# Seven blocks of transposing loads ahead of the stores, in a mixture-of-experts tail on one Trainium2 core

## The chip, the cores and the metric

The kernel runs on one core of one Trainium2 chip. The metric is the device time of one execution in microseconds (us); lower is better. The core has five engines with a sequencer each: PE (TensorE, matmuls, with its weight loads listed as PEld), DVE (VectorE), ACT (ScalarE), POOL (GpSimd) and SP (SyncE), which here only issues DMAs and waits on semaphores. A "q" behind an engine's name in a row (PEldq, SPq) marks an instruction of its sequencer.

## The reference

The input is x of 32 sequences of 256 tokens with 128 channels. Two layers are added to it in turn:

```
x = x + attn(layernorm(x))          # a gated linear recurrence (scan) with 192 channels
x = x + ffn(layernorm(x))           # the part below
def ffn(x):                         # 8192 tokens of 128 channels
    x = x + attention(layernorm(x)) # 16 heads of 8 channels, softmax over 256 keys
    m = layernorm(x)
    wts, idx = top_k(softmax(m @ Wg), 2)     # 2 of 8 experts for each token, weights normed
    h = gelu(m @ W1[e] + b1[e])              # 128 -> 512
    y = h @ W2[e] + b2[e]                    # 512 -> 128
    return x + sum over the 2 chosen experts of wts * y
```

## The kernel before, in words

The kernel goes through the scan layer, the attention of the first half of the sequences, the routing of that half, the attention and routing of the second half, and then the experts. This document is about the experts' stage, from about 818 us of the span to its end.

**Sorting by expert.** For each token and chosen expert POOL scatters a row into `xs` (expert_in) in DRAM with an indirect DMA, so that rows of one expert stand together. A row is 256 numbers of f16: the token's 128 channels as a high part and a low part. The rows are cut into `NBLK` = 80 blocks of `BS` = 256 rows, each of one expert, whose number stands in the table `blke`. Blocks 0 to 39 hold the first half of the tokens, 40 to 79 the second half. The second half's scatters still run while the first blocks are computed: POOL issues them as `down_done` counts up, and SP waits for all of them (`scattered[1]`) before its own block 32.

**One block.** SP loads the block with a transposing DMA into one of four buffers `XT[q]` (128 channels x 2 parts x 256 tokens, f16; it is a view of the tensor `arena`). PE makes `up(b)`: 12 matmuls of 256 columns with the expert's `w1h`, `w1l` into two PSUM banks. ACT makes `gelu(b)` in four instructions (line 854) into `G32`. DVE makes `split(b)`: a cast to f16 (line 1165) and a subtraction (line 1167). PE makes `down(b)`: 18 matmuls with `w2p` and the bias into a PSUM bank. DMA-ready output comes from one DVE reduction, `y_out(b)` (line 1172), into one of two buffers `YB`. SP stores it to `ys` (expert_out).

**The order on each engine** is written out by hand and runs over b with the helper `blocks`: blocks up to 3 and from 72 on are unrolled, and blocks 4 to 71 are a hardware loop with four blocks in a turn, q = 0 to 3. In its slot b each engine does the following.

- PE: reads the experts' numbers into registers (`value_load`, line 1476; two in slots q = 0, 1 and 2, one in q = 3), waits for `xt_in` of block b+3, for `gelu_done` of block b+1, for `gl_ready` of block b and for `yb_ready` of block b-2, and then issues `up(b+3)` and `down(b)` in turn. `up_done` and `down_done` are both raised at the slot's end. All of PE's matmuls go through one helper, line 1209.
- ACT: `gelu(b+2)`, as soon as `up(b+2)` is done.
- DVE: `y_out(b-1)`, which waits for `down(b-1)` and for the store of block b-3 to have landed, and then `split(b+2)`.
- SP: a load, then `store_block(b)`, which waits for `yb_ready`. All of SP's DMAs go into one queue.

The load in SP's slot b (line 446) is that of block b+4 into the buffer `XT[q]` that `up(b)` has read. It is issued behind `store_block(b-1)` (line 442), so behind `y_out(b-1)`. `exists(b)` is false only in the unrolled part for a block that there isn't.

**The end.** When all stores have landed, POOL gathers the second half's rows with 64 indirect DMAs (line 682), DVE combines them with `wts` and X, and SP stores the output. The first half's 64 gathers run beside blocks 41 to 78.

Of the kernel before, what the change touches and what calls it, by code (L numbers as in the profile page):

```python
# [63 lines left out]
def layer_kernel(nc, x, w_hg, b_hg, w_out, b_out, h0, g1, be1, g2, be2, wq, wk, wv, wo, wg, w1, b1,  # L64
# [8 lines left out]
    with ctx:  # L73
# [3 lines left out]
        def sem(name):  # L77
            return ctx.enter_context(nc.semaphore(name))
# [208 lines left out]
        up_done = sem("up_done")  # L287
# [30 lines left out]
        def blocks(eng, first, body, second_part=None):  # L318

            for b in range(first, 4):
                body(b, b % 4)
            cut = HBLK // 4 - 2
            for r0, r1 in ((1, cut), (cut, NBLK // 4 - 2)) if second_part else ((1, NBLK // 4 - 2),):
                if second_part and r0 == cut:
                    second_part()
                with eng.Fori(r0, r1) as r:
                    for q in range(4):
                        body(4 * r + q, q)  # L330
            for b in range(NBLK - 8, NBLK):
                body(b, b % 4)

        def exists(b):

            return not isinstance(b, int) or 0 <= b < NBLK
# [5 lines left out]
        def _(sp):  # L342
# [97 lines left out]
            def store_block(b, s):  # L440
                sp.wait_ge(yb_ready, b + 1)
                sp.dma_start(ys[bass.ds(b * BS, BS), :].rearrange("(h p) d -> p h d", p=P), YB[s])\  # L442
                  .then_inc(yb_out[s], 16)

            def load_block(b, q):
                sp.dma_start_transpose(XT[q], xs[bass.ds(b * BS, BS), :]).then_inc(xt_in[q], 16)

            def blocks_io(b, q):
                if exists(b + 4):
                    sp.wait_ge(up_done, b + 1)  # L450
                    load_block(b + 4, q)
                store_block(b, q % 2)

            sp.wait_ge(tab_ready, 2)
            sp.wait_ge(scattered[0], 32 * HN)
            for q in range(4):
                load_block(q, q)
            blocks(sp, 0, blocks_io, second_part=lambda: sp.wait_ge(scattered[1], 32 * (NT - HN)))

            for i in range(NG):  # L460
# [1116 lines left out]
```

## Time and profile before

| | us |
|---|---|
| median of 3 runs | 1243.0 |
| lowest and highest run | 1238.15, 1245.88 |
| the profiled execution's own time | 1232.73 |
| its span (first to last instruction) | 1230.9 |

| part of the span | us |
|---|---|
| before the experts | 0 to about 818 |
| expert blocks | about 818 to 1144 |
| gathers and combination of the second half | 1144 to 1230.9 |

PE is busy for 67% of the whole span, DVE for 70%, ACT for 49% and POOL for 37%. These are means over stages that differ, so they say little of the experts' stage. Rows give the time at which an instruction began and its duration; what stands in brackets behind a matmul is how long PE's array was idle before it and who is held to have ended that.

### The profile page before, as it was taken

Reading aid. Unit: us, or ns where it says so; the run is one execution under the profiler, and the core shown is the slowest. Engines: PE = TensorE matmul, PEld = TensorE weight load, DVE = VectorE, ACT = ScalarE, POOL = GpSimd, SP = SyncE. Lnnn points to the kernel's source line nnn. Section 1 sums busy time; section 2 is a strip of 40 time slices with the busy share of each in tenths; the row PEclk is TensorE's granted clock in tenths of the full one; section 3 lists DMA queues with packets and bytes.
Section 4 is the critical chain, followed back from the end, with each engine's and each line's share of the span. In section 5 each row is a group of like instructions: output and inputs, shape, how many; then the busy total and the mean of one; then the engine's idle time right before and its main releaser. Section 6 shows DMA issues by size and latency. Waiting matters only on the chain.

```text
span 1230.9 us, 25465 instructions
## 1 busy us (share of the span) xinstructions
PE 826.3 (67%) x8366; PEld 510.8 (41%) x8367; DVE 860.6 (70%) x1669; ACT 604.6 (49%) x1225; POOL 453.4 (37%) x552
## 2 busy tenths in 40 slices
PE   2577466688888884578888887547777777777000
PEld 1355344134443333423333333436666666666000
DVE  6788788777878847688888881856566666666722
ACT  3554278266767774227777775513333433343000
POOL 5800299011112214313333332724444033434675
PEclk9998799589989996559999997559999999999555
DMA  6900023211111210001211100013333233333432
GB/s 163 345 1 1 1 104 138 86 45 45 49 49 45 57 53 1 0 21 47 62 45 49 57 24 14 1 39 90 89 100 98 68 92 96 98 83 91 135 83 70
DMA packets 132071, 84.16 MB, mean 68 GB/s; under 512 B 54520, under 2 KB 117628, under 8 KB 131982
## 3 DMA queue, kind: packets, MB, share of 16 engines
q1 hardware_dynamic: 123790, 66.20, 18.6%
q0 software_dynamic: 8192, 16.79, 5.0%
q8 instruction: 54, 0.88, 0.3%
q14 instruction: 35, 0.29, 0.1%
HBM read 30.25 MB, written 41.94 MB: 59 GB/s over the span
## 4 chain that ended last, share of the span: by engine, by line
PE 44%; DVE 23%; POOL 9%; DMA 9%; issue 8%; ACT 4%; SPq 1%; ACTq 0%; DVEq 0%; POOLq 0%
PE bank L1209 41%; DVE arena L1024 9%; DMA arena<-expert_in 8%; POOL Z L682 2%; POOL HT L682 2%; POOL rr L473 2%; DVE arena L1172 2%; DVE mom L881 2%; POOL xh L477 2%; DVE arena L960 2%; PE bank L1389 1%; SPq L442 1%; ACT arena L854 1%; PE bank L1396 1%; PE bank L1213 1%
## 5 line engine op out<-in xcount | busy, mean ns | idle before, releaser
L1024 DVE TENSOR_REDUCE arena<-bank 128x2 f32<-128x512 f32 x512 | 337.3, 689 | 80.0 <-PE bank L1209 78.1
L774 ACT ACTIVATE arena<-bank 128x512 f32<-128x512 f32 x512 | 292.6, 596 | 131.2 <-PE bank L1209 128.1
L1209 PE MATMUL bank<-QK 32*128 32x256 f16 (+1 forms) x2048 | 204.8, 285 | 91.3 <-DVE arena L1024 69.2
L1209 PE MATMUL bank<-arena,w1h 128*128 128x256 f16 x640 | 170.9, 282 | 84.0 <-DMA arena<-expert_in 68.6
L640 POOL DMA_INDIRECT expert_in<-HT,idx x128 | 124.8, 975 | 266.7 <-PE bank L1209 239.2
L1209 PE MATMUL bank<-w2p,QK 128*128 x1280 | 221.6, 250 | 1.6 <-DVE arena L1172 1.6
L854 ACT ACTIVATE arena<-bank,b1s 128x256 f32<-128x256 f32 x320 | 125.5, 476 | 185.8 <-PE bank L1209 184.9
L1209 PEld LDWEIGHTS bank<-QK 31*128 31x128 f16 (+1 forms) x2048 | 63.3, 93 | 239.0 <-ACT arena L774 179.5
L1209 PE MATMUL bank<-arena,VA 128*32 128x256 f32 x2048 | 142.8, 398 | 1.4 <-ACT arena L774 1.4
L1209 PEld LDWEIGHTS bank<-w2p,QK 128*128 128x128 f16 x1280 | 126.0, 99 | 14.2 <-issue 1.7
L1209 PEld LDWEIGHTS bank<-arena,w1h 128*128 x640 | 64.2, 101 | 103.1 <-issue 96.8
L1165 DVE CAST QK<-arena 128x1024 f16<-128x1024 f32 x80 | 55.6, 696 | 70.4 <-ACT arena L854 70.4
L1213 PE MATMUL bank<-cst,xh 128*128 128x128 f32 x192 | 44.9, 386 | 86.7 <-ACT xh L813 32.6
L1167 DVE TENSOR_TENSOR QK<-arena,QK 128x1024 f16<-128x1024 f32 x80 | 98.0, 1226 | 2.7
L682 POOL DMA_INDIRECT Z<-expert_out,idx x64 | 61.9, 967 | 100.7 <-PE bank L1209 82.5
L473 POOL TENSOR_TENSOR rr<-vv,mhalf 128x8 f32<-128x8 f32 (+1 forms) x24 | 49.8, 2074 | 133.3 <-DVE vv L898 131.9
L1209 PE MATMUL bank<-arena,w1l 128*128 128x256 f16 x320 | 90.0, 281 | 0.0
L1172 DVE TENSOR_REDUCE arena<-bank 128x256 f32<-128x512 f32 x80 | 55.0, 689 | 44.1 <-PE bank L1209 42.2
L682 POOL DMA_INDIRECT HT<-expert_out,idx x64 | 62.0, 968 | 49.2 <-PE bank L1209 32.1
L1209 PEld LDWEIGHTS bank<-arena,VA 128*32 128x32 f32 x2048 | 54.7, 111 | 53.5 <-issue 23.2
L1213 PEld LDWEIGHTS bank<-cst,xh 128*128 128x128 f32 x192 | 31.3, 198 | 96.2 <-issue 49.4
L583 POOL COPY VA<-HT 128x128 f32<-128x128 f32 x64 | 16.8, 297 | 100.9 <-PE bank L1209 100.9
(150 smaller groups left out, 1220.4 us busy)
## 6 DMA issues: line engine op xcount, KB each, us to landing
QK<-qk_parts SPq DMA_DIRECT2D x96, 128.0 KB, 2.6
expert_in<-arena SPq DMA_DIRECT2D x40, 256.0 KB, 3.2
expert_out<-arena SPq DMA_DIRECT2D x80, 128.0 KB, 2.1
qk_parts<-arena SPq DMA_DIRECT2D x16, 512.0 KB, 2.8
X<-x SPq DMA_DIRECT2D x8, 512.0 KB, 5.8
wst<-w SPq DMA_DIRECT2D x16, 256.0 KB, 2.8
out<-arena SPq DMA_DIRECT2D x16, 256.0 KB, 2.4
expert_in<-HT,idx POOLq DMA_INDIRECT x128, 2.3
```

What stands on the lines that cost most here:

```text
L473: nc.gpsimd.tensor_tensor(rr[j % 2][:, 0:n, :], vv[j % 2][:, 0:n, :], mhalf[:, 0:n, :], ALU.pow)\
L477: return nc.gpsimd.tensor_scalar(dst, src, rr[j % 2][:, n, t:t + 1], nmr[j % 2][:, n, t:t + 1], ALU.mult, ALU.add)
L640: pool.indirect_dma_start(xs, bass.IndirectOffsetOnAxis(idx[:, k, n:n + 1], 0), MHL[:, n, :], None).then_inc(scattered[n // HN], 16)
L682: pool.indirect_dma_start(gat[k][:, n, :], None, ys[0:BS * BLK0[part + 1], :], bass.IndirectOffsetOnAxis(idx[:, k, n:n + 1], 0))\
L774: nc.scalar.activation(PT[t % 8], bank[2 + t % 2][:, :], ACT.Exp, scale=DH ** -0.5)\
L854: last = nc.scalar.activation(G32[s][:, BS * c:BS * c + BS], bank[2 + 2 * s + c // 2][:, BS * (c % 2):BS * (c % 2) + BS], ACT.Gelu_apprx_t ...
L1024: V.tensor_reduce(nmax[n % 2][:, :, 4 * j + g], bank[u % 2][:, :].rearrange("p (q t) -> p q t", q=2), AX.X, ALU.max, negate=True).then_inc ...
L1165: V.tensor_copy(GH[q], G32[q % 2]).then_inc(gh_own, 1)
L1167: V.tensor_tensor(GL[q], G32[q % 2], GH[q], ALU.subtract).then_inc(gl_ready, 1)
L1172: V.tensor_reduce(YB[s], bank[6 + s][:, :].rearrange("p (h k d) -> p h d k", h=2, k=2), AX.X, ALU.add) .then_inc(yb_ready, 1)
L1209: return nc.tensor.matmul(dst, lhsT, rhs, start=start, stop=stop)
L1213: last = nc.tensor.transpose(bk[:, P * t:P * t + P], src[:, t0 + t, :], ident)
```

## The change

SP sends its transposing loads earlier. Loads of blocks 0 to 6 are issued before the first store, blocks 4 to 6 each behind a wait for the buffer's last reader. In slot b the load is that of block b+7 into buffer (q+3) mod 4, behind a wait for `up(b+3)`, which reads that buffer last. The load still stands ahead of the store in the slot.

```
             def blocks_io(b, q):
-                if exists(b + 4):
-                    sp.wait_ge(up_done, b + 1)
-                    load_block(b + 4, q)
+                if exists(b + 7):
+                    sp.wait_ge(up_done, b + 4)
+                    load_block(b + 7, (q + 3) % 4)
                 store_block(b, q % 2)

             sp.wait_ge(tab_ready, 2)
             sp.wait_ge(scattered[0], 32 * HN)
-            for q in range(4):
-                load_block(q, q)
+            for b in range(7):
+                if b >= 4:
+                    sp.wait_ge(up_done, b - 3)
+                load_block(b, b % 4)
             blocks(sp, 0, blocks_io, second_part=lambda: sp.wait_ge(scattered[1], 32 * (NT - HN)))
```

The number of loads, their sizes, the four buffers and the one queue stay as they are.

## Rows read from the trace of the kernel before

**Rows 1.** The page: PE's clock in 40 slices, and the up-products' group.

```profile
PEclk9998799589989996559999997559999999999555
...
L1209 PE MATMUL bank<-arena,w1h 128*128 128x256 f16 x640 | 170.9, 282 | 84.0 <-DMA arena<-expert_in 68.6
```

**Rows 2.** Timeline of PE: first matmuls of slots 1 and 76.

```profile
832.43 0.28 PE L1209 MATMUL bank<-arena,w1h 128*128 128x256 f16 x1 [0.25 <-DVE QK L1167]
...
1131.80 0.28 PE L1209 MATMUL bank<-arena,w1h 128*128 128x256 f16 x1 [0.55 <-DMA arena<-expert_in]
```

**Rows 3.** Waits in 832 to 1132 us: total, times, longest.

```profile
PE bank L1209 <- DMA arena<-expert_in: 60.2, 62, 2.8
```

**Rows 4.** Timeline of PE: first matmuls of slots 32 to 37.

```profile
958.08 0.28 PE L1209 MATMUL bank<-arena,w1h 128*128 128x256 f16 x1 [1.80 <-ACT arena L854]
...
961.52 0.28 PE L1209 MATMUL bank<-arena,w1h 128*128 128x256 f16 x1 [0.51 <-DMA arena<-expert_in]
...
965.40 0.28 PE L1209 MATMUL bank<-arena,w1h 128*128 128x256 f16 x1 [0.95 <-DMA arena<-expert_in]
...
968.70 0.28 PE L1209 MATMUL bank<-arena,w1h 128*128 128x256 f16 x1 [0.37 <-DMA arena<-expert_in]
...
973.07 0.28 PE L1209 MATMUL bank<-arena,w1h 128*128 128x256 f16 x1 [1.45 <-DMA arena<-expert_in]
...
976.51 0.28 PE L1209 MATMUL bank<-arena,w1h 128*128 128x256 f16 x1 [0.50 <-DMA arena<-expert_in]
```

**Rows 5.** Timeline of SP: load of 36, store of 32, load of 37.

```profile
958.67 1.19 SPq L446 DMA_TRANSPOSE arena<-expert_in  x1
962.01 0.38 SPq L442 DMA_DIRECT2D expert_out<-arena  x1
962.61 1.19 SPq L446 DMA_TRANSPOSE arena<-expert_in  x1
```

**Rows 6.** Line 446, the loads, 832 to 1140 us: issue to landing.

```profile
DMA to landing us min/median/max: 2.6/2.9/4.5
```

**Rows 7.** Timeline of PE: last matmul of slot 32.

```profile
960.79 0.22 PE L1209 MATMUL bank<-b2h,ones 128*128 x1
```

**Rows 8.** Lines 1476, 1523, 958 to 973.2 us, PE's sequencer: ns, first, last.

```profile
L1476 PEldq TENSOR_LOAD <-blke x7: 297/302/310, 959.7 to 971.5; - x7
...
L1523 PEldq ALU_OP  x2: 32/34/36, 961.1 to 972.1; - x2
```

**Rows 9.** Line 316 (`used`), PE's sequencer, slot 33, then slot 34.

```profile
L316 PEldq EVENT_SEMAPHORE  x1: 51/51/51, 964.6 to 964.6; - x1
...
L316 PEldq EVENT_SEMAPHORE  x1: 51/51/51, 967.8 to 967.8; - x1
```

**Rows 10.** Timeline of PE: first matmuls of slots 47 and 48.

```profile
1015.36 0.28 PE L1209 MATMUL bank<-arena,w1h 128*128 128x256 f16 x1 [0.87 <-DMA arena<-expert_in]
...
1019.30 0.28 PE L1209 MATMUL bank<-arena,w1h 128*128 128x256 f16 x1 [1.01 <-DVE arena L1172]
```

**Rows 11.** Lines in 832 to 1132 us, DVE: busy, mean ns, idle before.

```profile
L1167 DVE TENSOR_TENSOR QK<-arena,QK 128x1024 f16<-128x1024 f32 x76 | 93.1, 1226 | 2.6
L1172 DVE TENSOR_REDUCE arena<-bank 128x256 f32<-128x512 f32 x76 | 52.4, 689 | 42.3 <-PE bank L1209 42.2
L1165 DVE CAST QK<-arena 128x1024 f16<-128x1024 f32 x75 | 52.2, 696 | 60.5 <-ACT arena L854 60.5
```

**Rows 12.** Timeline of ACT: the gelu after slot 32.

```profile
961.03 1.57 ACT L854 ACTIVATE arena<-bank,b1s 128x256 f32<-128x256 f32 x4 [3.09 <-PE bank L1209]
```

**Rows 13.** Timeline of PE: first matmuls of slots 68 and 69.

```profile
1098.32 0.28 PE L1209 MATMUL bank<-arena,w1h 128*128 128x256 f16 x1 [2.21 <-DMA arena<-expert_in]
...
1102.65 0.37 PE L1209 MATMUL bank<-arena,w1h 128*128 128x256 f16 x1
```

**Rows 14.** Windows: busy time of each engine, granted clock, DMA share, GB/s.

```profile
870.00:910.00 40.00, 29.70 (x305) 25.36 (x303) 26.96 (x32) 15.79 (x41) 19.19 (x20) 1.00 0.38 101
...
1098.00:1103.00 5.00, 4.68 (x33) 3.77 (x34) 1.83 (x3) 0.22 (x1) 0.71 (x1) 0.66 0.33 79
```

**Rows 15.** Line 442, the stores, 832 to 1145 us: issue to landing.

```profile
DMA to landing us min/median/max: 1.8/2.1/2.6
```

**Rows 16.** Timeline of POOL: first gather of the second half.

```profile
1144.53 0.94 POOL L682 DMA_INDIRECT Z<-expert_out,idx  x1 [5.40 <-DMA expert_out<-arena]
```

## Prediction, on record before the changed kernel was built

> **What bounds the kernel now.** I read the waits of the experts' stage first, then PE's timeline slot by slot, then PE's sequencer. The page's group of the up-products already says it: before them PE stood idle for 84.0 us, of which 68.6 ended with a load [rows 1]. In 832 to 1132 us, 75 slots from slot 1 to slot 76 [rows 2], PE waited 62 times for a load, 60.2 us in all [rows 3]. These slots take 1131.80 - 832.43 = 299.4 us, 3.99 each.
>
> The timeline shows how. The load of block 36 is issued at 958.67 and slot 33, which needs it, starts at 961.52, 2.85 later; that of block 37 is issued at 962.61 and slot 34 starts at 965.40, 2.79 later [rows 4, 5]. The loads land 2.6 to 4.5 us after issue, 2.9 in the median [rows 6]. So PE starts as the load lands. The load in turn is late because it stands behind a store in SP's order: the store of block 32 goes out at 962.01, the load 0.60 behind it [rows 5], and the store waits for `y_out`. After a slot ends, reduction, store, load and landing follow, 0.7 + 0.2 + 0.6 + 2.9 = 4.4 us, before the slot after the next can start. In slot 32 the first and last matmuls start at 958.08 and 960.79 [rows 4, 7]: the array needs 2.71 us plus one spacing of 0.06, so 2.77 a slot. That is what a reader might take as the new pitch, and it would be wrong, I think, by the next finding.
>
> **PE's sequencer is nearly as slow as the loads.** Slot 32 lasts 3.44 (958.08 to 961.52), slot 36 again 3.44 (973.07 to 976.51) [rows 4], and so do nine of the fourteen first-of-four slots from 12 to 64, whatever time the load was issued. A wait on a DMA does not repeat to 0.01 us. What repeats is the sequencer's own work between two slots: register arithmetic for the matmuls' addresses, then the reading of experts' numbers into registers, seven times in the group of slots 32 to 35, each 0.30 us [rows 8] plus some 0.45 of arithmetic and check about it, and the loop's branch. I take its time in each kind of slot from its last instruction ahead of the next slot. In slot 32 line 1523 runs at 961.1, 0.4 before the next slot starts [rows 4, 8]. In slot 33 the sequencer reaches its wait of line 316 at 964.6, in slot 34 at 967.8 [rows 9]; that is 3.1 and 2.4 after the slot's start, and 0.2 more pass from there to the first matmul (slot 32: line 1523 at 961.1, 0.1 to line 1527, 0.1 to line 316, 0.2 to 961.52). A slot of the fourth kind has the branch: slot 35 starts at 968.70 and line 1523 runs at 972.1, 3.4 later [rows 4, 8], and 0.4 to 0.5 follow. Slot 47 shows the whole: 1015.36 to 1019.30, 3.94 [rows 10]. So the four kinds cost the sequencer 3.44, 3.3, 2.6 and 3.94: **13.3 us for four blocks**, 3.32 each. Only the third kind is shorter than the array's 2.77, and there the sequencer runs 0.17 ahead and keeps it.
>
> **The change part by part.**
>
> The load's wait. The load of block b+7 goes out at the end of slot b and is needed at the start of slot b+4. Three slots lie between, 3 x 3.32 = 10.0 us, against 4.5 for the slowest landing [rows 6]. So all 62 waits of rows 3 should go. What is late next is the sequencer: 75 slots are 18.75 groups, 18.75 x 13.3 = 249.4 us, against 299.4. **Gain 50.0 us.** That is less than the 60.2 of waiting, since in slots of the first and fourth kind the wait lay beside sequencer work that stays.
>
> The other waits of PE's slot, at the new pitch. The gelu starts 0.03 after the slot's end and takes 1.57 [rows 12]; PE wants it one slot later, so 1.7 are left. DVE has 0.69 + 0.70 + 1.23 = 2.61 us of work in a slot of 3.32 [rows 11]. Its split ends 1.6 + 0.1 + 0.7 + 1.23 = 3.6 after the slot's end, so `y_out` begins some 0.3 late each time; PE asks for it, and for the split, a whole slot later. Cost 0; if the cover were gone it would be this 0.3 in each slot, 20 us.
>
> SP's added wait and the moved load. Each slot's load now waits for `up_done` of this very slot, and behind it in SP's order stand the store of block b and all later loads. `up_done` and `down_done` rise together, and the store needs `y_out` behind `down_done` anyway (0.69, [rows 11]). The load's issue takes 1.19 [rows 5], so the store goes out at about 1.5 us after the slot's end, up to 0.5 later than without the load. It lands 2.1, at most 2.6 later [rows 15], at 4.1; `y_out` wants the buffer two slots on, at 6.6. So 2.5 us of cover. SP has 1.19 + 0.38 of issue and under 1 us of steps in a slot: no bound. If a store's data queued behind the load's, even its worst landing of 4.5 [rows 6] would give some 6.2, still in time.
>
 No row of before has a store that close behind a load. By that rule the store would land at about 6 us, and the sum would stay at 50.0 us.
>
> The start and blocks 4 to 6. Slots before 832.43 did not wait for a load beyond the first; cost and gain 0. The scatters of the second half: 56 of them are released by 29 down-products, one per 1.72 us at the new pitch, and POOL needs about 1.25 for such a DMA (0.94 and a gap of 0.3, as in the gathers, [rows 16]). They keep up, and SP's wait before slot 32 would find three more blocks loaded. The tail from 1144.53 on, 64 gathers, hangs on the last store and only moves with it: 0.
>
> The clock. It is at 0.9 or more in the slices of this stage [rows 1], 1.00 (2.4 GHz) in 870 to 910 and 0.66 in 1098 to 1103, so partly at 1.2 GHz [rows 14]; slot 68 there takes 4.33 [rows 13] instead of 3.44, and slots 4, 8 and 72 are of this sort. These stretches came behind PE's longest pauses in the stage. I take them as gone, which the 13.3 already holds; if they stay, 4 x 0.9 = 3.6 us are lost.
>
> **Sum.** 1232.7 - 50.0 = 1182.7 for the profiled execution. The median of the runs is 1243.0, 10.3 above it, and I expect this distance again: **1193 us**. Own range: a group at 13.0 (0.3 of it being misread steps) gives 1187, one at 13.7 with the slow-clock slots 1204.
>
> **Rivals.**
>
> The array bounds (chance 0.05). If the sequencer's work were hidden because it runs ahead, a slot would be 2.77 to 2.82: 75 x 1.19 = 89 us less, 1154. For it: in slots of the third kind it does run ahead. Against it: an in-order sequencer needs 13.3 for four blocks whatever its lead, and 3.44 repeats. The skill's page TensorE: Matmul & The Clock Gate (section on the array as 16 of 32×32) gives PE a queue of 64, which lets it run that far ahead; by this alone the array would set the pace. The rows decide for me: depth hides a delay, not a lower rate.
>
> A new wait takes half of it (0.15). `y_out` waits for stores that land late, or DVE's lag of 0.3 grows through gelu and split. A pitch of 3.65, halfway between 3.32 and 3.99, gives 1243 - 25 = 1218. For it: three engines then have under 1 us of slack per slot. Against it: the slacks above of 1.7, 2.5 and more.
>
> The loads are not what ends the waits (0.05). Slot 32 starts 0.1 behind the end of a gelu by its label [rows 4]; if PE truly waited for the newest gelu, nothing would move: 1243. Against it: the code asks for a gelu one slot older, and slots 33 to 35 carry the load's label.
>
> Slower (0.04): stores behind loads in one queue. A store's landing L sets a pitch of (0.7 + 0.5 + L) / 2, since `YB` has two buffers. It costs something from L = 5.4 on (3.32 x 2 - 1.2), and all of the gain and more from 6.8 on. With L = 7.5 the pitch is 4.35: 75 x 0.36 = 27 us more, 1270. Against it: 2.6 at most now [rows 15], and DMA engines that are busy for 0.38 [rows 14], which the denser stage would raise to 0.46.
>
> **Chances.** Forecast 0.70, the array 0.05, half of it 0.15, nothing 0.05, slower 0.04, other 0.01. Range: the forecast's own and the rival at 1218 with its bounds, 1183 to 1222; the array's case, nothing and slower stay out, 0.14. This kernel can't tell changes under about 1% from none. Faster by over 1%: 0.91; within: 0.05; slower: 0.04.
>
> **What would show it.** Right: hardly a wait of PE for `expert_in`, slots of 3.44, 3.3, 2.8 and 3.8 in turn, slots 1 to 76 in about 250 us, the idle time before the up-products ended by nothing but issue. Loads landing 5 us or more before use. Wrong: a pitch of 2.8 (array), DVE's reduction ended by `expert_out` DMAs (stores), equal pitches of 3.6 with labels of ACT or DVE, or a granted clock below 1.00 in mid-stage.

## The result, and the profile after

| | before | changed |
|---|---|---|
| median, us | 1244.44 (4 runs, 1238.15 to 1251.02) | 1194.6 (4 runs, 1192.46 to 1201.33) |
| profiled execution's own time | 1232.73 | 1193.93 |
| its span | 1230.9 | 1192.1 |

The ratio is 0.9608, with a 95% interval of 0.9544 to 0.9672: 49.8 us faster by the medians, against 50.0 on record. That closeness is partly luck. The span fell by 38.8 only, and the parts of it, below, tell which terms were right. Medians here are of all executions of a kernel; ratios and their intervals leave out executions over 1.5% above the kernel's fastest.

The page and the waits of the expert stage come first. Behind the edit, lines of the kernel have moved by two: 1211 is the helper through which all of PE's matmuls go, 1169 DVE's subtraction, 1174 its reduction.

```profile
span 1192.1 us, 25516 instructions
...
L1211 PE MATMUL bank<-arena,w1h 128*128 128x256 f16 x640 | 167.6, 277 | 49.3 <-DVE QK L1169 24.9
```

Waits in 834 to 1089 us of the changed kernel (total, times, longest):

```profile
PEld bank L1211 <- issue: 47.4, 58, 1.4
...
PE bank L1211 <- DVE QK L1169: 24.9, 36, 1.1
...
PE bank L1211 <- issue: 11.4, 20, 1.0
```

No wait for `expert_in` is left of the 62 with 60.2 us in [rows 3]. The pauses of PE that are left carry the label of a DVE subtraction or "issue", which stands for time in which the engine waited for nothing that the profile shows; an experiment below tests the first of these labels. The timeline of PE, first matmuls of slots 1, 32 to 37 and 76, which answer to [rows 2, 4]:

```profile
834.24 0.28 PE L1211 MATMUL bank<-arena,w1h 128*128 128x256 f16 x1 [0.25 <-issue]
...
941.11 0.28 PE L1211 MATMUL bank<-arena,w1h 128*128 128x256 f16 x1 [1.00 <-DVE QK L1169]
...
944.55 0.28 PE L1211 MATMUL bank<-arena,w1h 128*128 128x256 f16 x1 [0.51 <-issue]
...
947.96 0.28 PE L1211 MATMUL bank<-arena,w1h 128*128 128x256 f16 x1 [0.48 <-DVE QK L1169]
...
950.72 0.27 PE L1211 MATMUL bank<-arena,w1h 128*128 128x256 f16 x1
...
954.64 0.28 PE L1211 MATMUL bank<-arena,w1h 128*128 128x256 f16 x1 [1.00 <-DVE QK L1169]
...
958.11 0.28 PE L1211 MATMUL bank<-arena,w1h 128*128 128x256 f16 x1 [0.54 <-issue]
...
1088.47 0.28 PE L1211 MATMUL bank<-arena,w1h 128*128 128x256 f16 x1 [0.60 <-issue]
```

The four kinds of slot take 3.44, 3.41, 2.76 and 3.92 us here. Only behind the third does the array go on without a pause. Slots 1 to 76 take 1088.47 - 834.24 = 254.2 us, 3.39 each, against 299.4. PE's sequencer (line 1525 is 1523 of before) in 941 to 956 us:

```profile
L1525 PEldq ALU_OP  x2: 32/34/36, 944.1 to 954.1; - x2
```

In slot 32 it gets to that line 3.0 us after the slot's start, in slot 35 at 3.4, as in [rows 8]. Its work takes as long as before; what is gone is the wait for loads that lay over it. SP's timeline for two slots:

```profile
940.14 1.19 SPq L446 DMA_TRANSPOSE arena<-expert_in  x1
941.64 0.38 SPq L442 DMA_DIRECT2D expert_out<-arena  x1
944.07 1.19 SPq L446 DMA_TRANSPOSE arena<-expert_in  x1
945.53 0.38 SPq L442 DMA_DIRECT2D expert_out<-arena  x1
```

Each load goes out at the end of a slot, its store 1.5 us behind it, as forecast. DVE's reduction hardly waits any more, and not for stores; the clock is full in the whole stage (0.98 in 832 to 1132 us before). DVE's reduction and the stage as a window, 834 to 1089 us (behind the window's length stand the busy times of PE, PEld, DVE, ACT and POOL with their instructions, then the granted clock, the DMA engines' busy share and GB/s):

```profile
L1174 DVE TENSOR_REDUCE arena<-bank 128x256 f32<-128x512 f32 x76 | 52.2, 687 | 3.9 <-PE bank L1211 2.8
```

```profile
834.00:1089.00 255.00, 217.41 (x2256) 189.04 (x2257) 192.36 (x227) 118.90 (x304) 119.84 (x116) 1.00 0.41 106
```

So the stage gave 299.4 - 254.2 = 45.2. Slot 1 began 1.8 later, and from slot 76 to the end 1192.1 - 1088.47 = 103.6 went by against 99.1 before, 4.5 more. 45.2 - 1.8 - 4.5 = 38.9, the difference of the spans up to rounding.

### The profile page after: what moved, and what is told of

Same layout as the page of the kernel before. It is cut to its first block, busy times and chain, and to the rows that moved or that the text cites. A ratio compares the mean times of both kernels' runs of the same rounds, so it can differ in the third digit from the quotient of the medians.

```text
span 1192.1 us, 25516 instructions
## 1 busy us (share of the span) xinstructions
PE 817.4 (69%) x8366; PEld 507.0 (43%) x8367; DVE 857.5 (72%) x1669; ACT 604.7 (51%) x1225; POOL 460.7 (39%) x552
## 4 chain that ended last, share of the span: by engine, by line
PE 47%; DVE 25%; POOL 12%; issue 9%; ACT 4%; DMA 1%; ACTq 1%; another core or an unknown queue 0%; SPq 0%; POOLq 0%; DVEq 0%
PE bank L1211 44%; DVE arena L1026 9%; POOL rr L475 3%; POOL xh L479 3%; DVE QK L1169 3%; POOL HT L684 2%; POOL Z L684 2%; ACT arena L856 2%; DVE arena L962 2%; DVE mom L883 2%; DVE QK L1167 2%; PE bank L1391 1%; PE bank L1398 1%; DVE xh L1080 1%; ACT arena L776 1%
## 5 line engine op out<-in xcount | busy, mean ns | idle before, releaser
L1211 PE MATMUL bank<-w2p,QK 128*128 x1280 | 215.8, 246 | 1.6 <-DVE QK L1169 1.6
L1211 PE MATMUL bank<-arena,w1h 128*128 128x256 f16 x640 | 167.6, 277 | 49.3 <-DVE QK L1169 24.9
L1211 PEld LDWEIGHTS bank<-w2p,QK 128*128 128x128 f16 x1280 | 124.0, 98 | 12.9 <-issue 1.7
L1215 PE MATMUL bank<-cst,xh 128*128 128x128 f32 x192 | 44.9, 386 | 88.1 <-ACT xh L815 32.6
L475 POOL TENSOR_TENSOR rr<-vv,mhalf 128x8 f32<-128x8 f32 (+1 forms) x24 | 49.8, 2076 | 132.8 <-DVE vv L900 131.4
L1169 DVE TENSOR_TENSOR QK<-arena,QK 128x1024 f16<-128x1024 f32 x80 | 98.0, 1226 | 2.7
L684 POOL DMA_INDIRECT Z<-expert_out,idx x64 | 64.3, 1005 | 79.4 <-PE bank L1211 60.9
L684 POOL DMA_INDIRECT HT<-expert_out,idx x64 | 64.8, 1013 | 37.5 <-PE bank L1211 19.0
L1215 PEld LDWEIGHTS bank<-cst,xh 128*128 128x128 f32 x192 | 31.3, 198 | 97.6 <-issue 49.5
```

The costliest lines, as they stand in the source:

```text
L475: nc.gpsimd.tensor_tensor(rr[j % 2][:, 0:n, :], vv[j % 2][:, 0:n, :], mhalf[:, 0:n, :], ALU.pow)\
L684: pool.indirect_dma_start(gat[k][:, n, :], None, ys[0:BS * BLK0[part + 1], :], bass.IndirectOffsetOnAxis(idx[:, k, n:n + 1], 0))\
L1169: V.tensor_tensor(GL[q], G32[q % 2], GH[q], ALU.subtract).then_inc(gl_ready, 1)
L1211: return nc.tensor.matmul(dst, lhsT, rhs, start=start, stop=stop)
L1215: last = nc.tensor.transpose(bk[:, P * t:P * t + P], src[:, t0 + t, :], ident)
```

## The experiments

There are twelve experiments, two of them repeats. A kernel's stage is the time from the first matmul of slot 1 to that of slot 76, its tail what comes behind. The runs went to three chips: the first four experiments below to one on which the kernel before had a median of 1240.28, the two with one reading more, the first unrolled run and the last experiment to one with 1240.69, the other four to one with 1235.14. Each ratio is to the kernel before on the same chip, and the stage is what is best compared between chips. The kernel before itself was profiled once.

**The changed kernel again.** No edit.

> The changed kernel once more, for a second profile. Both theories: 1195 us. The first profile lost 4.5 us behind the last expert slot and 1.8 ahead of slot 1 against the profile of before, at places where semaphores were seen 3 to 4 us late. If that belongs to the change it comes again at the same places; if it is an accident of one execution it is elsewhere or gone, and the span is up to 6 us shorter.

1197.89 us, ratio 0.9657 (0.9608 to 0.9706). The stage is 252.2 (835.82 to 1087.99), the span 1193.9, the tail 105.9. The waits of the tail (1087 to 1194 us):

```profile
DVE arena L1203 <- remote: 26.1, 6, 4.5
DVE arena L1195 <- remote: 18.8, 5, 4.5
```

"remote" stands for a wait to whose end the trace shows no releaser. Most of it costs nothing, since DVE would wait for gathers anyway: in the kernel before its waits for them in the tail are 47.4 us. POOL is done with the last gather 92.8 us after the first matmul of slot 76, and 92.3 in the kernel before; DVE's last combination ends at 103.1, against 96.4. In the first profile of the changed kernel one long wait of this kind stands in the tail, of 3.0 us, ahead of the very last combination. It is not the queue's doing: the experiment below that keeps the queue of before has it too, and the runs on the third chip don't. So the longer tail comes again, 105.9 here and 103.6 there, with its waits at places that vary, and not because of the change.

**A shorter lead.**

```
-                if exists(b + 7):
-                    sp.wait_ge(up_done, b + 4)
-                    load_block(b + 7, (q + 3) % 4)
+                if exists(b + 5):
+                    sp.wait_ge(up_done, b + 2)
+                    load_block(b + 5, (q + 1) % 4)
...
-            for b in range(7):
+            for b in range(5):
```

> Loads five blocks ahead instead of seven. A load is then issued about 1.3 us after the end of slot b-1 and needed at the start of slot b+2, 5.4 us later at a pitch of 3.4, against 2.9 for a landing. Sequencer theory (PE's sequencer sets the pitch once loads are not late): same as with seven, 1195 us. Rival (what helps is the long lead, since landings scatter up to 4.5 us): waits for loads come back, 1205 to 1220 us.

1206.23 us, ratio 0.9692 (0.9611 to 0.9774), which can't be told from 0.9657. The stage is 254.5 (843.46 to 1098.00), and one wait for a load is left in it:

```profile
PE bank L1211 <- DMA arena<-expert_in: 0.9, 1, 0.9
```

The profile's longer span comes mostly from before the experts: slot 1 started 9.2 us later than in the first profile of the changed kernel. At this pitch one block more of lead than before does all, within what these runs can tell, that three do.

**The store ahead of the load.**

```
             def blocks_io(b, q):
+                store_block(b, q % 2)
                 if exists(b + 7):
                     sp.wait_ge(up_done, b + 4)
                     load_block(b + 7, (q + 3) % 4)
-                store_block(b, q % 2)
```

> Seven blocks ahead, but the store of block b stands ahead of the load of block b+7. Sequencer theory: 1195 us, since neither store nor load ends a wait of PE or DVE. Rival (stores suffer behind the loads in the one queue): 5 us or more faster, and the store's landing, seen in what waits for it, earlier.

1199.43 us, ratio 0.9667 (0.9606 to 0.9729), stage 254.7. No difference that these runs could show: a store issued 0.3 us behind the issue of a load costs this kernel nothing. When the store lands doesn't stand in the profile.

**Less work for DVE.**

```
-                V.tensor_tensor(GL[q], G32[q % 2], GH[q], ALU.subtract).then_inc(gl_ready, 1)
+                V.tensor_tensor(GL[q][:, 0:2 * BS], G32[q % 2][:, 0:2 * BS], GH[q][:, 0:2 * BS], ALU.subtract)\
+                    .then_inc(gl_ready, 1)
```

> DVE subtracts for the first half of the columns of each block only, so the low part of half the hidden values is left out; DVE has 0.6 us less to do per slot. The waits after the change name this instruction as what ended PE's idle time, 36 times. Sequencer theory: the name is a coincidence of time, 1195 us. Rival (PE now waits for DVE's split): the pitch falls by 0.3 to 0.6 us, 1150 to 1172 us.

1195.59 us, ratio 0.9634 (0.9586 to 0.9683). The stage is 251.6 (856.83 to 1108.46, at a granted clock of 1.00; the profiled execution took 1214.38 us and came to slot 1 22.6 us later than the first profile of the changed kernel, with a granted clock of 0.83 up to there instead of 0.87). It is no shorter than the 252.2 of the same changed kernel beyond what profiles differ by, though DVE's subtraction went from 1226 ns to 692:

```profile
L1169 DVE TENSOR_TENSOR QK<-arena,QK 128x512 f16<-128x512 f32 x75 | 51.9, 692 | 2.6
```

The stage kept its pitch, and PE's idle time stayed, 34.5 us against 37.6, under other labels. These are its waits (lines have moved by one more: 1212 is PE's helper, 1175 the reduction):

```profile
PE bank L1212 <- issue: 23.8, 45, 1.0
PE bank L1212 <- DVE arena L1175: 8.0, 8, 1.1
PE bank L1212 <- DVE QK L1169: 2.7, 3, 1.3
```

The 24.9 us under the subtraction's name were a coincidence of time.

**One reading more per slot, changed kernel.** In PE's `experts`, the function of its slot:

```
                     if exists(x) and k not in known:
                         known[k] = expert_of(x)
+                if exists(b):
+                    expert_of(b)
```

> The changed kernel with one more reading of an expert's number into a register of PE in each slot; the result isn't used. Sequencer theory: 0.30 for the reading and 0.45 for what stands about it come on top of each slot, four blocks take 13.3 + 3.0 = 16.3 us, 75 slots 56 us more: 1251 us. Rival (DVE, ACT or the array sets the pitch, and the sequencer runs ahead): 1195 us, at most 10 more.

1241.87 us, ratio 1.0037 (1.0008 to 1.0067): one more reading per slot takes the whole gain back. First matmuls of slots 1 and 76:

```profile
835.17 0.28 PE L1211 MATMUL bank<-arena,w1h 128*128 128x256 f16 x1 [0.91 <-DVE QK L1169]
...
1134.85 0.28 PE L1211 MATMUL bank<-arena,w1h 128*128 128x256 f16 x1 [0.90 <-DVE QK L1169]
```

299.7 - 254.2 = 45.5 us more in 75 slots, 0.61 each where 0.75 was expected. PE's array, DVE, ACT and the DMAs have nothing more to do, so this shows the sequencer as the bound. The waits' table names ACT and DVE for most of the new idle time (29.6 and 41.1 us). Those labels name whoever finished last before the sequencer came.

**The same in the kernel before.** The same two lines.

> The same additional reading in the kernel before. Sequencer theory: slots of the first kind go from 3.44 to 4.19, the others hide part of it beside their wait for a load; 10 to 25 us more than before, 1254 to 1270 us, clearly less than the 56 in the changed kernel. Rival (loads alone set the pitch before): 1244 us.

1252.7 us, ratio 1.008 (1.0049 to 1.011). The stage went from 299.4 to 306.1, 6.7 more (840.47 to 1146.53); by the time 12. So the same work costs little while loads are the bound, less than I expected in the stage. What it comes to is the slower of the two paths: in slots 12 to 67 four blocks take 16.3 us here and 16.1 in the changed kernel with the same reading, so with it the sequencer is the slower path in most slots of the kernel before too. In its tail, with the queue of before:

```profile
DVE arena L1201 <- remote: 22.0, 7, 4.5
```

**PE's order unrolled, changed kernel.** Each expert's number is read once.

```
-                if q == 0:
-                    known.clear()
-                for x, k in ((u, q + 3), (b, q)):
-                    if exists(x) and k not in known:
-                        known[k] = expert_of(x)
+                for x in (u, b):
+                    if exists(x) and x not in known:
+                        known[x] = expert_of(x)
...
-            blocks(pe, -3, experts)
+            for b in range(-3, NBLK):
+                experts(b, b % 4)
```

> The changed kernel with PE's order unrolled in full: each expert's number is read once, 83 readings instead of 140 and no branch. Sequencer theory: a slot costs the sequencer some 2.6 us, less than the array's 2.77, so the array sets the pitch at 2.8: 75 x 0.58 = 43 us less than the changed kernel, 1152 us, unless fetching the longer program costs something. Rival (DVE or ACT sets the pitch): 1195 us.

1164.41 us, ratio 0.938 (0.9278 to 0.9482), and the stage 223.3, so 31 us less than the changed kernel where 43 were expected. Waits without a releaser now stand in the stage itself (832 to 1055 us), above all ACT's for the up-products:

```profile
ACT arena L856 <- remote: 50.8, 24, 3.4
```

One such place, around slot 12:

```profile
864.99 0.22 PE L1211 MATMUL bank<-b2h,ones 128*128 x1
865.04 0.27 PE L1211 MATMUL bank<-arena,w1h 128*128 128x256 f16 x1
...
866.68 0.27 PE L1211 MATMUL bank<-arena,w1h 128*128 128x256 f16 x1 [0.53 <-issue]
867.00 1.19 SPq L446 DMA_TRANSPOSE arena<-expert_in  x1
867.04 0.69 DVE L1174 TENSOR_REDUCE arena<-bank 128x256 f32<-128x512 f32 x1 [0.63 <-remote]
867.07 1.57 ACT L856 ACTIVATE arena<-bank,b1s 128x256 f32<-128x256 f32 x4 [3.01 <-remote]
```

SP, DVE and ACT wait there for the end of slot 11, whose last matmul is recorded at 864.99, and all three go on only at 867.00 to 867.07; and PE itself stood still for 0.53 us within slot 12, where its program waits for nothing. So something held up PE's sequencer or its signals in this run. What it was these traces don't show.

> The changed kernel with PE's order unrolled once more, in more rounds, to time it well. 1164 us; slots of 2.74 for most of the time with some of 3.1 to 3.8 between, pitch 2.98.

The same program on the third chip: **1139.19 us, ratio 0.9234 (0.9188 to 0.9281)**, not one wait of that kind in the stage, and none of PE. First matmuls of slots 1, 26 to 28 and 76:

```profile
833.43 0.27 PE L1211 MATMUL bank<-arena,w1h 128*128 128x256 f16 x1
...
902.62 0.27 PE L1211 MATMUL bank<-arena,w1h 128*128 128x256 f16 x1
905.37 0.27 PE L1211 MATMUL bank<-arena,w1h 128*128 128x256 f16 x1
908.11 0.27 PE L1211 MATMUL bank<-arena,w1h 128*128 128x256 f16 x1
...
1039.05 0.27 PE L1211 MATMUL bank<-arena,w1h 128*128 128x256 f16 x1
```

Every slot takes 2.74 or 2.75 us, the stage 205.6: the array without a gap. Its tail is 99.3 with the changed queue, once more with no "remote" wait. This version beats both kernels.

**The unrolled kernel with less work for DVE** (the two edits together).

> The unrolled kernel with the subtraction of DVE for half of the columns only (the low part of half the hidden values is left out). Theory: the 0.2 us by which the unrolled kernel's pitch lies above the array's 2.74 are stalls of PE's sequencer and of semaphores, and DVE, busy for 85% of the stage, isn't the bound: 1164 us, within 5. Rival (DVE now sets part of the pitch): 10 to 16 us faster, 1150.

1138.85 us, ratio 0.9217 (0.9166 to 0.9269), against 1139.19 for the unrolled kernel on the same chip, and the stage 205.6 again. DVE is busy for 92% of the stage of the unrolled kernel (189.17 of 206 us) and still not its bound.

**No reading at all, still a loop.**

```
-                        known[k] = expert_of(x)
+                        known[k] = 0
```

> The changed kernel, still a loop, but PE reads no expert's number and uses expert 0 for all blocks, so the results are those of the wrong expert; the amount of work is the same. Sequencer theory: four blocks cost the sequencer 13.3 less 7 readings of 0.75, 8.1 us and less arithmetic, so the array sets the pitch at 2.75 to 2.8, as good as unrolled or better: 45 us less than the changed kernel, 1152 us. If the branch counts by itself, the fourth kind of slot stays above 3 us. Rival (the readings are hidden, what unrolling took away was the branch): 1180 us or more.

1142.08 us, ratio 0.9247 (0.9183 to 0.931), stage 205.6, every slot at 2.74 or 2.75, the fourth kind too. So the loop's branch does not count by itself. But this edit takes away more than the readings. With the expert fixed at 0 the addresses of the weights are constants, and the register arithmetic for them goes as well. In the changed kernel four slots have these instructions in PE's sequencer (941 to 954.6 us); here there are none of them in the whole stage:

```profile
L1211 PEldq FUSED_REGOPS  x37: 46/46/46, 941.0 to 954.5; - x37
L1211 PEldq ALU_OP  x16: 32/32/32, 941.4 to 952.1; - x16
```

So it shows that the sequencer's work for the experts' numbers, reading and arithmetic together, is what held the loop back, and not which part. By the 0.61 us that one added reading cost, the seven readings of four blocks are about 4.3 us, an estimate, more than the 2.6 by which 13.6 lies above the array's 11.0, so they alone would do. The unrolled kernel keeps the arithmetic for the weights and has three readings fewer in four blocks, 1.8 us by the same price. The rest of its 2.6, at least 0.8, then came from what else unrolling took away, the loop's own register work and the branch; this was not tried apart.

**The unrolled kernel with the shorter lead.**

> The unrolled kernel with loads five blocks ahead instead of seven. At a pitch of 2.8 a load still has 4.3 us from issue to need, against 2.9 for a landing, but 4.5 for the slowest. If the median landing decides: 1164 us. If the slow landings do: some waits for loads come back, 1167 to 1180.

1161.16 us, ratio 0.9412 (0.9359 to 0.9465). The times on record were set from the 1164 us of the other chip; here seven blocks took 1139.19, so five are 22 us slower, and it is the second case. The stage is 220.4, and waits for loads are back (831 to 1052 us):

```profile
PE bank L1211 <- DMA arena<-expert_in: 10.1, 13, 1.5
```

The stage is 14.8 us longer. Measured from the last matmul's start to the next slot's first, the thirteen pauses with this label hold 12.9 us where the gapless kernel has 0.7, and other short pauses most of the rest. The profiled execution is only 12.3 us above that of the unrolled kernel (1152.39 against 1140.11); what the three slower ones spent beyond it was not traced. The landings of these loads don't stand in the profile. That at a pitch of 2.74 a lead of two slots no longer covers the slow ones of up to 4.5 us [rows 6] is the reading that fits.

**The unrolled order in the kernel before.** The edit of the unrolled kernel, with the queue of before.

> The same unrolling in the kernel before. Two slots then take the 4.4 us from a slot's end to the landing of the load, plus a slot's 2.77 and 0.1: 7.3, a pitch of 3.64 against 3.99. Sequencer theory: 26 us less than before, 1218 us. Rival (only the loads counted in the kernel before): 1244 us.

1260.41 us, ratio 1.0142 (1.0037 to 1.0247): **slower** by 1.4%, with 0.4 to 2.5% in the interval, where 26 us less were expected. The stage is 318.8 against 299.4, 19.5 more. Four slots in a stretch at full clock, the stage's windows, and its wait for loads:

```profile
935.74 0.28 PE L1209 MATMUL bank<-arena,w1h 128*128 128x256 f16 x1 [1.58 <-DMA arena<-expert_in]
939.62 0.28 PE L1209 MATMUL bank<-arena,w1h 128*128 128x256 f16 x1 [0.95 <-DMA arena<-expert_in]
943.53 0.28 PE L1209 MATMUL bank<-arena,w1h 128*128 128x256 f16 x1 [0.98 <-DMA arena<-expert_in]
947.41 0.28 PE L1209 MATMUL bank<-arena,w1h 128*128 128x256 f16 x1 [0.95 <-DMA arena<-expert_in]
```

```profile
837.00:1156.00 319.00, 235.81 (x2255) 199.66 (x2252) 195.26 (x227) 118.03 (x302) 115.71 (x116) 0.94 0.35 87
```

```profile
PE bank L1209 <- DMA arena<-expert_in: 77.1, 54, 3.1
```

Two things were wrong. One is the load's path, which makes a pitch of 3.9 by itself: slots 20 to 43 took 3.92 in the mean, against 3.83 in the kernel before and 3.64 on record. From the end of a slot's last matmul to the start of the slot after the next 4.87 us pass in the mean of these slots: 0.22 until DVE's reduction starts (at most 1.21, where its split comes first), 0.69 for it, 0.89 to the load's issue, and 3.07 from there. I had 0.7, 0.8 and 2.9, so 4.4; the kernel before has 4.74. So in the kernel before the sequencer's 3.3 lay under the loads' 3.8, in the mean of four slots.

The other is the clock: eleven of the 75 slots ran partly at 1.2 GHz (granted clock 0.62 to 0.65), 4.0 to 4.5 us from first to last matmul instead of 2.7, where the kernel before has four. This is the larger part of the 19.5 us: the matmul time of the 75 slots, first to last, sums to 221.3 us against 209.8, and the pauses between slots to 97.6 against 89.6. The granted clock of the stage fell to 0.94 from 0.98. Every slow slot stands behind a pause of PE of 2.1 us or more, from one matmul's start to the next; there are 13 such pauses here and 6 in the kernel before. But two of the 13 and two of the 6 brought no slow slot, nor did the two in the kernel before with one reading more (2.7 and 2.3 us), whose clock was 1.00 in the stage and whose median pause, 1.4 us, is the same as here. That a faster sequencer leaves longer pauses beside the same loads, and that these brought the slow slots, is a reading that fits; it was not tried by itself.

## Why the prediction was right

**The loads' wait goes: right.** 60.2 us of waits became none, and SP's rows are those forecast. How long before use the loads now land doesn't stand in the profile.

**What is late next is PE's sequencer: right, and now shown.** Adding one reading gave 45.5 us, taking the readings away together with the weights' address arithmetic brought the stage to the array's pace, and halving DVE's subtraction did nothing. One of the signs came out otherwise: the idle time before the up-products was to end by nothing but issue, and 24.9 us of it bore a DVE name, which the experiment showed to mean nothing. "The array bounds" was the rival that a look at busy times suggests; it came true only in the unrolled and the reading-free kernels.

**The size of the stage's term: 45.2 instead of 50.0.** The term that was mis-sized is the group of four, 13.3 us on record. Slots 12 to 67 measure 3.50, 3.43, 2.78 and 3.90, 13.6 in all. The second profile has 3.46, 3.39, 2.77 and 3.92. I had taken the third kind at the sequencer's 2.6, as if its lead of 0.17 over the array would shorten the next slot, which kept its 3.9; and the second kind at 3.3.

**The start and the tail at 0: 6.3 us short in the profile.** They are no effect of the change. Of the 1.8 us at the start 1.75 lie in one slot, the one before slot 0, which took 4.13 against 2.38; it took 4.18 and 3.98 in the two experiments with the queue of before, and 1.7 to 2.1 with the changed queue on the third chip. The tail was 105.1 and 103.7 in the same two, and 98.5 to 99.3 on the third chip. The 99.1 of the profile of before was the short case.

**The distance to the median: wrong, and it made up for both.** I added 10.3 us to the profiled time since the profiled execution of before lay so far below its median. After the change it was 0.7 (1193.93 to 1194.6). By the steps alone 1182.7 was forecast for the profiled execution, which took 11.2 more: 4.8 in the stage, 6.3 outside it. That the median came within 2 us of the 1193 is luck to that extent. What the other executions of the kernel before spent beyond the profiled one, which is faster than all four timed ones, stays open.

**The store behind the load: right at cost 0.** Putting it first changed nothing. The rule of the Trainium skill's page DMA: Bandwidth & Descriptors (section Queues, rings and completion order), that descriptors are consumed in ring order, is neither borne out nor refuted by that. The stores' landings don't stand in these profiles; whatever the queue adds stayed within the cover, on record as 2.5 us, since in the stage no reduction waited for a store. That a store would have to wait for the load's data was my own step from that rule.

**The slow clock gone: right.** The granted clock was 1.00 in the stage.

## What to carry to other kernels

When a wait is to be removed, look for what repeats to the hundredth of a microsecond beside it: here a slot of 3.44 us told of the sequencer behind the loads, and priced the gain at 50 where the waits said 60 and the array's pace 89; the stage gave 45. One more reading of a value from memory into a register of PE cost 0.61 us a slot, seen as "issue" or under the name of any engine that happened to finish then. Read each value once, and test a label by changing the work it names. The lead of a prefetch has to be judged at the pitch that the next improvement gives: five blocks did at 3.39 us a block and not at 2.74.

## What the runs showed of the hardware that was not expected

- Waits whose end no releaser in the trace explains, up to 4.5 us long, on two of the three chips of the experiments: 44.9 us of them at DVE in one tail, most of it beside gathers, and 50.8 at ACT in one expert stage, where PE also stood still within slots. The same unrolled program was 1164.41 us on a chip that showed them and 1139.19 on one that didn't. Their cause was not found, and they come with either order of the queue.
- A faster sequencer made a load-bound kernel slower, 1260.41 against 1240.69, with TensorE's granted clock at 0.94 instead of 0.98 over the stage.
